# Decoder layer on one core: rotated queries and keys spread to head slots by four SBUF-to-SBUF transfers a group instead of four ScalarE copies

## The chip, the cores and the metric

The kernel is written directly in engine instructions and runs on 1 core of one Trainium2 chip. TensorE (PE), VectorE (DVE), ScalarE (ACT), GpSimd (POOL) and SyncE (SP) each run a list of their own and meet at semaphores. SP issues most transfers. The metric is the device time in microseconds of one execution; less is better.

## The reference, cut to what matters

128 sequences of 64 tokens with 128 features go through self-attention with rotary positions (16 heads of 8 dimensions, causal), cross-attention without softmax, and a feed-forward part that sends every token to one of 8 experts. Only the first part is touched:

```python
qkv = x @ qkv_w.T + qkv_b                       # after a layer norm of x
q, k, v = (qkv[0], qkv[1], qkv[2])              # 16 heads x 8
q = apply_rope(q, cos, sin)                     # pairs dimension d with d + 4 of its head
k = apply_rope(k, cos, sin)
scores = jnp.einsum('bhqd,bhkd->bhqk', q, k) / math.sqrt(Hd)
scores = jnp.where(causal, jnp.finfo(scores.dtype).min, scores)
attn = jax.nn.softmax(scores, axis=-1)
out = jnp.einsum('bhqk,bhkd->bhqd', attn, v)
```

## The kernel before

The 8192 tokens are cut into 32 groups of 256 (NG = 32). A first part runs over groups as a pipeline: every engine has a function `one(g)`, which lists its steps for one round, and `stage(g, k, step)` runs a step for group g - k. So in round r the first steps work on group r and the last ones on group r - 8. Within an engine the list is fixed, and a step that waits holds up all behind it. Nearly every tile is double (`two(...)`), chosen by the parity of the group. A second part runs 71 blocks of 128 rows through the experts; in it PE is the busiest engine. Nothing of this second part is changed.

For one group the front of the pipeline is: load `xin` (SP, `load_x`), row statistics (DVE, `stats_x`), scale (POOL `std_x`, ACT `norm_x`), turn (PE, ACT `xT`), queries and keys (PE `queries_keys`, L661), bias and rotation factors (DVE `rotate`, L1389), exchange of the rotary partners between partitions (DVE `partners`, L1399), and the difference `qk` (POOL `rotated`, L1885). `qk` is 128 x 512: features on partitions, 256 tokens of queries and 256 of keys.

A matmul for scores takes a strip of 32 partitions, that is four heads. To tell the heads apart, one operand is `ex`, 128 x 4 x 512: slot i holds the rows of `qk` that belong to head i of their strip, and zeros elsewhere. Before the change ACT makes it with four instructions a group (`by_head`, L1048), each a copy of the whole `qk` scaled by a column of zeros and ones (`own4`). Slots 2 and 3 are made one ACT round later than 0 and 1. PE reads `ex` in `max_scores` (L690, whose row maxima DVE takes at L1409) and in `scores` (L723); L728 adds the shifts and ACT takes the exponential (`exp`, L1064, `prob`).

SP's list for a round is `load_x` of group r, `load_ctx` of group r, `load_again` of group r - 3, then late constants in the first rounds, the mask in round 4 (`LOAD_AT`) and an expert weight of 256 KB in each of rounds 10 to 25. The three loads wait for the buffer to be free: `load_x` for `norm_x` of two groups before, `load_ctx` for the turn of the context (L755), `load_again` for `x1`.

POOL's list for a round is `std_x`, `std_y` (L1931 to L1935), `divide` (L1900), `rotated` (L1885), `max_low` (L1892), two indirect stores of rows (`scatter_rows`, L1980, which wait for the slot numbers `sli` that DVE makes at L1603 after `turned_back` at L1432 and `scaled_scores` at L1494), `std_x2` (L1948 to L1952), `row_scalars`, `offset_x1` (L1923), `std_x1` (L1911 to L1916), `gain` (L1940) and `scaled_affinity` (L1970).

Of the kernel before, what the change touches and what calls it, by code (L numbers as in the profile page):

```python
# [35 lines left out]
P = 128  # L36
# [108 lines left out]
def decoder_kernel(nc, x, ctx, mask, wself, wcross, bcol, brow, cent, w1t, lngb, b1c, w2t, b2r,  # L145
# [17 lines left out]
    with es:  # L163
# [10 lines left out]
        ws = sb("ws", [P, 6, D])  # L174
        WQ, WQR, WK, WKR, WV, WO = (ws[:, i, :] for i in range(6))
        wcx = sb("wcx", [P, 4 * D + E])
# [19 lines left out]
        o += P  # L196
        own4, own4s = cf[:, o:o + 4], cf[:, o + 4:o + 8]
        o += 8
# [144 lines left out]
        ac_l = stage_steps("act_norm_x", "n")  # L343
        ac_f = stage_steps("act_front", "xT | V0 V1 | x0 x1 x2 x3 | hi")
        ac_a = stage_steps("act_exp", "e0 | e1")
# [15 lines left out]
        d_xr = [sem(f"dma_x_again{i}") for i in range(2)]  # L361
        d_c = [sem(f"dma_ctx{i}") for i in range(2)]
        d_s = [sem(f"dma_scatter{i}") for i in range(2)]
        d_ident = sem("dma_identity")
# [15 lines left out]
        s_gain = sem("setup_routing_weights")  # L380
        s_turn = sem("setup_turned_weights")
        s_masks = sem("setup_scalar_masks")
        s_pads = sem("pad_rows_known")
# [76 lines left out]

        N_CONST, N_BIAS, N_LATE, N_WEIGHTS = 3, 10, 4, 2 * E
        LOAD_AT, WEIGHTS_AT = 4, 10
# [14 lines left out]
        def _(sp):  # L477
# [47 lines left out]
            def load_ctx(g):  # L525
# [4 lines left out]
                             ).then_inc(d_c[g.par], 16)  # L530

            def one(g):
                stage(g, 0, load_x)
                stage(g, 0, load_ctx)
                stage(g, 3, load_again)
# [38 lines left out]
        def _(pe):  # L574
# [80 lines left out]
            def queries_keys(g):  # L655

                first(pe, g, s_centre, 1)
                wait(pe, ac_f, g.n, "xT")
                free(g, "queries_keys")
                for i, w in enumerate((WQ, WK)):  # L660
                    last = mm(BANK["queries_keys"][:, i * TG:(i + 1) * TG], w, xT[g.par][:, :], start=True, stop=True)  # L661
                last.then_inc(*pe_f.done("QK"))
                if g.n == 1:
                    constants()
# [10 lines left out]
            def max_scores(g):  # L675

                first(pe, g, s_zero, 4)
                first(pe, g, s_masks, 1)
                for r_ in range(4):
                    free(g, f"max_scores{r_}")  # L680
                    half_ = slice(64 * (r_ % 2), 64 * (r_ % 2) + 64)
                    mm(quad[:, r_, :], ii[half_, :, :].rearrange("p b k -> p (b k)"), negq_b[half_, :],
                       start=True, stop=False, tile_position=(64 * (r_ % 2), 0))
                wait(pe, ac_f, g.n, "x3")
                for j in range(J):
                    for b in range(2):
                        own = slice((2 * j + b) * SQ, (2 * j + b + 1) * SQ)
                        for r_ in range(4):
                            strip = slice(32 * r_, 32 * r_ + 32)
                            last = mm(quad[64 * b:64 * b + 64, r_, 256 * j:256 * j + 256],  # L690
                                      qk[g.par][strip, 0, own], ex[g.par][strip, :, 1, own],
                                      start=False, stop=j == J - 1, tile_position=(32 * r_, 64 * b))
                            if j == J - 1 and b == 1:
                                last.then_inc(*pe_s.done(f"s{r_}"))
# [15 lines left out]
            def scores(g):  # L710
# [4 lines left out]
                for r_ in range(4):  # L715
                    free(g, f"scores{r_}")
                wait(pe, ac_f, g.n, "x3")
                for j in range(J):
# [269 lines left out]
        def _(ac):  # L988
            act, cp = nc.scalar.activation, nc.scalar.copy

            def masks():

                ac.wait_ge(d_rope, 32)
                cp(bvx[:, :], bc[:, 5:6].broadcast_to((P, P)))
                cp(pick[0:64, :, :, :].rearrange("p c b k -> p (c b) k"),
                   identf[0:64, 0:64].unsqueeze(1).broadcast_to((64, 8, SQ)))
                ac.wait_ge(d_const, 16 * N_CONST)
                for i in range(2):
                    cp(shift[i][0:64, :, :, :].rearrange("p j i q -> p (j i) q"),
                       nkf[0:64, :].unsqueeze(1).broadcast_to((64, 4 * J, SQ)))  # L1000
                cp(tri_b[:, :], trif)
                cp(negq_b[:, :].rearrange("p (h k) -> p h k", k=SQ),
                   nqf[:, :].unsqueeze(1).broadcast_to((P, 512 // SQ, SQ))).then_inc(s_masks, 1)
# [26 lines left out]
            def max_by_head(g):  # L1030
# [8 lines left out]
                last.then_inc(*ac_s.done("x"))  # L1039

            def by_head(g, part_):

                first(ac, g, d_const, 16 * N_CONST)
                wait(ac, pe_s, g.n - 2, "s3")
                wait(ac, pe_a, g.n - 2, "s3")
                wait(ac, po_f, g.n, "qk")
                for i in part_:
                    act(ex[g.par][:, i, :, :].rearrange("p a t -> p (a t)"),  # L1048
                        qk[g.par][:, :, :].rearrange("p a t -> p (a t)"), ACT.Copy, scale=own4[:, i:i + 1]
                        ).then_inc(*ac_f.done(f"x{i}"))  # L1050

# [130 lines left out]
            def one(g):  # L1182
                stage(g, 3, by_head, (2, 3))
                stage(g, 5, norm_x1)
# [11 lines left out]
                stage(g, 6, token_ids)  # L1196
                stage(g, 2, by_head, (0, 1))
                stage(g, 3, exp, 0)
# [4 lines left out]
            ac.dma_start(cf[:, i0:i1], consts[:, i0:i1]).then_inc(d_ident, 16)  # L1203
            ac.dma_start(cf[:, 0:i0], consts[:, 0:i0]).then_inc(d_rope, 16)
            ac.dma_start(bc[:, :], bcol).then_inc(d_rope, 16)
            ac.wait_ge(s_pool, 1)
# [51 lines left out]
        def _(dv):  # L1258
# [112 lines left out]
            def stats_x(g):  # L1371
# [3 lines left out]
                if g.n == 0:  # L1375
                    identities()
                    dv.wait_ge(s_pe, 1)
                    v.tensor_tensor(ws[:, 0:5:2, :], ws[:, 0:5:2, :],
                                    M[0][:, 0:3 * D].rearrange("p (a d) -> p a d", d=D), ALU.subtract
                                    ).then_inc(s_centre, 1)  # L1380

            def rotate(g):

                first(dv, g, d_rope, 32)
                wait(dv, po_f, g.n - 2, "qk")
# [9 lines left out]
            def partners(g):  # L1395
# [4 lines left out]
                                 t2[g.par][:, :, :].rearrange("p a t -> p (a t)"),  # L1400
                                 [p ^ (HD // 2) for p in range(32)]).then_inc(*dv_f.done("sh"))
                if g.n == 1:
# [281 lines left out]
            def setup(i):  # L1684
# [15 lines left out]
                v.tensor_scalar(pen[:, :], pen[:, :], 0.0, 1.0, ALU.mult, ALU.add).then_inc(s_mask, 1)  # L1700

            rounds(one, NG + 4, early=setup)

# [155 lines left out]
        def _(po):  # L1859
# [19 lines left out]
            def rotated(g):  # L1879

                wait(po, ac_f, g.n - 2, "x3")
                wait(po, pe_s, g.n - 2, "s3")
# [119 lines left out]
            for k in range(2):  # L2002
                v.memset(sc[k][:, :, 2], 1.0)
            v.memset(ones_b[:, :], 1.0).then_inc(s_pool, 1)
            po.wait_ge(s_pool, 1)

# [130 lines left out]
```

## Time and profile before

| | |
|---|---|
| median of 3 runs | 604.65 us (603.29 to 607.4) |
| the profiled execution | 602.47 us |
| its span | 600.2 us |
| busy: PE, DVE, ACT, POOL | 528.8, 496.4, 492.7, 421.1 us |
| mean granted TensorE clock | 0.989 of full speed |
| moved by DMA | 35.35 MB, 59 GB/s |

The span is the time between the first and the last instruction of the trace; 2.27 us of the profiled execution lie around it. A start in the rows is counted from the start of the span. "idle before" in square brackets is the time for which the engine stood still before the first instruction of a row, with what ended it. SPq and ACTq are the issue of a transfer by the queue of SP and ACT.

### The profile page before, as it was taken

What the parts mean: (1) busy time and instruction counts of PE and PEld (TensorE: products, weight loads), DVE (VectorE), ACT (ScalarE), POOL (GpSimd) and SP (SyncE); (2) the same over time, 40 slices, a digit from 0 to 9 for tenths busy, and PEclk for the clock granted to TensorE, in tenths of its full rate; (3) what the DMA queues carried; (4) which work ended last, traced back from release to release, by engine and by line L of the source; (5) the groups of instructions that cost most, each with busy time, mean ns of one, the idle gap of its engine ahead of it and who ended that gap; (6) DMA issues with size and microseconds to landing.
All of it is one profiled execution on the core that took longest, in us unless ns stands there. A gap on an engine that the chain in (4) does not pass through costs nothing.

```text
span 600.2 us, 25006 instructions
## 1 busy us (share of the span) xinstructions
PE 528.8 (88%) x7951; PEld 410.0 (68%) x7951; DVE 496.4 (83%) x1762; ACT 492.7 (82%) x1358; POOL 421.1 (70%) x820
## 2 busy tenths in 40 slices
PE   2755999999999988999989999898879998999995
PEld 1533776666666666666666666666668898899994
DVE  3627899999999999999999999999768777777773
ACT  1735788988988888888888888888778797899993
POOL 1311568888888888888888888887757766555553
PEclk9996999999999999999999999999999999999999
DMA  5142112122122111232211211110301222322210
GB/s 150 41 57 52 29 35 63 43 58 55 56 78 88 57 55 56 66 92 63 56 56 57 59 52 39 38 38 22 86 21 56 70 64 72 98 74 67 68 53 14
DMA packets 55183, 35.35 MB, mean 59 GB/s; under 512 B 14977, under 2 KB 50434, under 8 KB 55057
## 3 DMA queue, kind: packets, MB, share of 16 engines
q1 hardware_dynamic: 50160, 24.44, 15.6%
q0 software_dynamic: 4320, 8.66, 4.3%
q8 instruction: 68, 1.11, 0.8%
q10 hardware_dynamic: 576, 0.66, 0.4%
q14 instruction: 59, 0.48, 0.3%
HBM read 24.46 MB, written 9.74 MB: 57 GB/s over the span
## 4 chain that ended last, share of the span: by engine, by line
POOL 31%; PE 29%; issue 22%; DVE 10%; ACT 2%; DMA 2%; DVEq 2%; POOLq 1%; SPq 0%; ACTq 0%
PE side L940 8%; POOL expert_rows L1980 6%; POOL pay L1952 4%; PE quad L925 4%; PE side L925 4%; POOL on L1900 3%; POOL rs_T L1914 3%; POOL x L1923 3%; POOL rs_L L1875 2%; DVE hT L1551 2%; PE side L661 1%; PE quad L909 1%; PE quad L690 1%; DMA mk<-in_mask 1%; POOL ve_L L1873 1%
## 5 line engine op out<-in xcount | busy, mean ns | idle before, releaser
L2013 POOL DMA_INDIRECT out<-yo,rb x71 | 70.1, 987 | 60.1 <-DVE yo L1757 53.8
L1980 POOL DMA_INDIRECT expert_rows<-pay,sli x64 | 65.5, 1024 | 33.9 <-DVE sli L1603 19.6
L1048 ACT ACTIVATE ex<-qk,cf 128x512 f32<-128x512 f32 x128 | 85.4, 721 | 0.1
L1409 DVE TENSOR_REDUCE mx<-quad 128x16 f32<-128x1024 f32 x64 | 77.5, 1219 | 4.5 <-PE quad L690 4.1
L940 PE MATMUL side<-w,hT 128*128 x568 | 76.8, 278 | 4.7 <-DVE hT L1551 3.1
L940 PEld LDWEIGHTS side<-w,hT 128*128 128x128 f32 x568 | 69.1, 192 | 7.6 <-issue 7.3
L1064 ACT ACTIVATE prob<-quad 128x1024 f32<-128x1024 f32 x64 | 65.8, 1032 | 3.0 <-PE quad L728 2.2
L1541 DVE TENSOR_SCALAR xh<-rb 128x128 f32<-128x128 f32 x71 | 25.2, 356 | 28.2 <-issue 23.3
L1088 ACT ACTIVATE xn<-x,mr,rs_T 128x128 f32<-128x128 f32 x64 | 28.1, 486 | 24.3 <-POOL mr L1916 24.1
L1161 ACT COPY w1b<-w 128x512 f32 x71 | 43.5, 615 | 0.3 <-issue 0.3
L1009 ACT ACTIVATE xn<-xin,rs_L 128x128 f32<-128x128 f32 x64 | 22.2, 394 | 24.8 <-POOL rs_L L1875 24.7
L1036 ACT ACTIVATE shift<-side,own_i 64x128 bf16<-64x128 f32 x128 | 36.1, 355 | 2.8 <-PE side L704 1.1
L925 PE MATMUL quad<-xhT,w1b 128*128 128x128 f32 x288 | 38.2, 276 | 0.0
L690 PE MATMUL quad<-ex,qk 32*64 32x256 f32 x1024 | 36.1, 387 | 1.5 <-ACT ex L1048 1.5
L742 PE MATMUL side<-prob,vau 128*32 128x64 f32 x2048 | 35.7, 221 | 1.9 <-ACT prob L1064 1.8
L925 PE MATMUL side<-xhT,w1b 128*128 128x128 f32 x280 | 37.2, 276 | 0.0
L723 PE MATMUL quad<-ex,qk 32*64 32x256 f32 x1024 | 36.4, 392 | 0.4 <-DVE vau L1307 0.4
L925 PEld LDWEIGHTS quad<-xhT,w1b 128*128 128x128 f32 x288 | 35.4, 193 | 0.1
L661 PE MATMUL side<-xT,ws 128*128 128x256 f32 x128 | 34.9, 397 | 0.6 <-ACT xT L1016 0.6
L1952 POOL TENSOR_TENSOR pay<-ve,half 128x4 f32<-128x4 f32 x32 | 33.3, 1041 | 2.7
L1169 ACT ACTIVATE bs<-rb 128x128 f32<-128x128 f32 x71 | 35.0, 493 | 0.0
L1139 ACT ACTIVATE xhT<-quad,gb 128x128 f32<-128x128 f32 x71 | 33.0, 465 | 2.0 <-PE quad L909 1.8
(270 smaller groups left out, 1634.1 us busy)
## 6 DMA issues: line engine op xcount, KB each, us to landing
rb<-expert_rows SPq DMA_DIRECT2D x71, 68.0 KB, 1.9
xin<-in_x SPq DMA_DIRECT2D x32, 128.0 KB, 3.3
cin<-in_ctx SPq DMA_DIRECT2D x32, 128.0 KB, 2.1
xr<-in_x SPq DMA_DIRECT2D x32, 128.0 KB
w<-in_w1t SPq DMA_DIRECT2D x8, 256.0 KB, 3.6
w<-in_w2t SPq DMA_DIRECT2D x8, 256.0 KB, 3.4
out<-yo,rb POOLq DMA_INDIRECT x71
expert_rows<-pay,sli POOLq DMA_INDIRECT x64, 2.9
```

The source lines that it names most:

```text
L661: last = mm(BANK["queries_keys"][:, i * TG:(i + 1) * TG], w, xT[g.par][:, :], start=True, stop=True)
L690: last = mm(quad[64 * b:64 * b + 64, r_, 256 * j:256 * j + 256], qk[g.par][strip, 0, own], ex[g.par][strip, :, 1, own], start=False, stop= ...
L723: mm(quad[64 * b:64 * b + 64, r_, 256 * j:256 * j + 256], qk[g.par][strip, 1, own], ex[g.par][strip, :, 0, own], start=j == 0, stop=False, ...
L925: last = mm(HT[u][c // 2][:, (c % 2) * P:(c % 2 + 1) * P], w1b[u][:, c * P:(c + 1) * P], xhT[u][:, :], start=True, stop=True)
L940: last = mm(YB[u][:, 0:D], hT[u][:, c, :], w2[:, bass.ds(e, 1), c, :], start=c == 0, stop=c == FC - 1)
L1048: act(ex[g.par][:, i, :, :].rearrange("p a t -> p (a t)"), qk[g.par][:, :, :].rearrange("p a t -> p (a t)"), ACT.Copy, scale=own4[:, i:i + ...
L1064: act(prob[g.par][:, 2 * h_:2 * h_ + 2, :], quad[:, 2 * h_:2 * h_ + 2, :], ACT.Exp).then_inc(*ac_a.done(f"e{h_}"))
L1161: cp(w1b[u][:, :], w1[:, bass.ds(e, 1), :].rearrange("p e f -> p (e f)")).then_inc(*ffn["act_w1"].done("act_w1"))
L1409: v.tensor_reduce(mx[g.par][:, 2 * h_:2 * h_ + 2, :], quad[:, 2 * h_:2 * h_ + 2, :].rearrange("p r (h k) -> p r h k", k=SQ), AX.X, ALU.max ...
L1952: v.tensor_tensor(px[:, :, C_RS:C_A + 1], ve2[g.par][:, :, :], half[:, :].rearrange("p (j a) -> p j a", a=2), ALU.pow).then_inc(*po_r.done ...
L1980: v.indirect_dma_start(out=rows, out_offset=bass.IndirectOffsetOnAxis(ap=sli[g.par][:, j:j + 1], axis=0), in_=pay[g.par][:, j, :], in_offs ...
L2013: v.indirect_dma_start(out=o_rows, out_offset=bass.IndirectOffsetOnAxis(ap=number, axis=0), in_=yo[b.c % 4][:, :], in_offset=None, bounds_ ...
```

## The change

The four ACT copies a group are taken out. SP issues four transfers a group instead: slot i of `ex` gets the partitions i, i + 4, i + 8, ... of `qk`, 32 rows of 2 KB each. For that the features of queries and keys are laid out in another order within each strip of 32: the dimension first and the head last, so that head i has the rows i, i + 4, ... The two weight matrices get this order when DVE subtracts their mean, the rotary partner is now 16 partitions away instead of 4, and the rotation factors and biases are loaded in the new order (ten transfers on ACT's queue instead of two). The zeros of `ex` are written once, at the start, one buffer by DVE and one by POOL.

```diff
@@ SP
+            def by_head(g):
+                first(sp, g, s_clear, 2)
+                wait(sp, pe_s, g.n - 2, "s3")
+                wait(sp, pe_a, g.n - 2, "s3")
+                wait(sp, po_f, g.n, "qk")
+                for i in range(4):
+                    sp.dma_start(ex[g.par][i:P:4, i, :, :], qk[g.par][i:P:4, :, :]).then_inc(d_by[g.par], 16)
             def one(g):
+                stage(g, 2, by_head)
                 stage(g, 0, load_x)
                 stage(g, 0, load_ctx)
                 stage(g, 3, load_again)
@@ PE: queries_keys, and max_scores and scores
-                for i, w in enumerate((WQ, WK)):
+                for i, w in enumerate((WQP, WKP)):
...
-                wait(pe, ac_f, g.n, "x3")
+                wait_dma(pe, d_by, g, 4)
@@ ACT
-            def by_head(g, part_):
-                first(ac, g, d_const, 16 * N_CONST)
-                wait(ac, pe_s, g.n - 2, "s3")
-                wait(ac, pe_a, g.n - 2, "s3")
-                wait(ac, po_f, g.n, "qk")
-                for i in part_:
-                    act(ex[g.par][:, i, :, :].rearrange("p a t -> p (a t)"),
-                        qk[g.par][:, :, :].rearrange("p a t -> p (a t)"), ACT.Copy, scale=own4[:, i:i + 1]
-                        ).then_inc(*ac_f.done(f"x{i}"))
...
-                stage(g, 3, by_head, (2, 3))
...
-                stage(g, 2, by_head, (0, 1))
...
-            ac.dma_start(cf[:, 0:i0], consts[:, 0:i0]).then_inc(d_rope, 16)
-            ac.dma_start(bc[:, :], bcol).then_inc(d_rope, 16)
+            for r_ in range(4):
+                own = slice(32 * r_, 32 * r_ + 32)
+                ac.dma_start(cf[own, 0:4 * SQ], consts[own, 0:4 * SQ].rearrange("(i m) c -> m i c", i=4)
+                             ).then_inc(d_rope, 16)
+                ac.dma_start(bc[own, 0:4], bcol[own, 0:4].rearrange("(i m) c -> m i c", i=4)).then_inc(d_rope, 16)
+            ac.dma_start(cf[:, 4 * SQ:i0], consts[:, 4 * SQ:i0]).then_inc(d_rope, 16)
+            ac.dma_start(bc[:, 4:6], bcol[:, 4:6]).then_inc(d_rope, 16)
@@ DVE: stats_x of group 0, partners, and the start
-                    v.tensor_tensor(ws[:, 0:5:2, :], ws[:, 0:5:2, :],
-                                    M[0][:, 0:3 * D].rearrange("p (a d) -> p a d", d=D), ALU.subtract
-                                    ).then_inc(s_centre, 1)
+                    for i, w in enumerate((WQP, WKP)):
+                        v.tensor_tensor(w.rearrange("p (r m i) -> p r i m", r=4, i=4),
+                                        ws[:, 2 * i, :].rearrange("p (r i m) -> p r i m", r=4, i=4),
+                                        M[0][:, i * D:(i + 1) * D].rearrange("p (r i m) -> p r i m", r=4, i=4),
+                                        ALU.subtract)
+                    v.tensor_tensor(WV, WV, M[0][:, 2 * D:3 * D], ALU.subtract).then_inc(s_centre, 1)
...
-                                 [p ^ (HD // 2) for p in range(32)]).then_inc(*dv_f.done("sh"))
+                                 [p ^ 16 for p in range(32)]).then_inc(*dv_f.done("sh"))
...
+            v.memset(ex[0][:, :, :, :], 0.0).then_inc(s_clear, 1)
@@ POOL: rotated, and the start
-                wait(po, ac_f, g.n - 2, "x3")
+                wait_dma(po, d_by, g.back(2), 4)
...
+            v.memset(ex[1][:, :, :, :], 0.0).then_inc(s_clear, 1)
```

Three places show what this does to the lists. The first is SP's list in two rounds of the middle of the first part, before:

```order
L514 DMA xin_1<-in_x 128x2x128 [waits act_norm_x_n]
L528 DMA cin_1<-in_ctx 128x2x128 [waits pe_cross_cT]
L521 DMA xr_0<-in_x 128x2x128 [waits dve_cross_x1]
L509 DMA w2<-in_w2t 128x512
L514 DMA xin_0<-in_x 128x2x128 [waits act_norm_x_n]
```

and after:

```order
L515 DMA xin_1<-in_x 128x2x128 [waits act_norm_x_n]
L529 DMA cin_1<-in_ctx 128x2x128 [waits pe_cross_cT]
L522 DMA xr_0<-in_x 128x2x128 [waits dve_cross_x1]
L510 DMA w2<-in_w2t 128x512
L540 DMA ex_0<-qk_0 32x512 [waits pool_front_qk,pe_attention_s0,pe_scores_for_max_s0]
L540 DMA ex_0<-qk_0 32x512 x3
L515 DMA xin_0<-in_x 128x2x128 [waits act_norm_x_n]
```

Each load of `xin` now stands behind the four transfers of the group two before, and so behind that group's `qk`. The second place is the head of ACT's list, before:

```order
L1202 DMA ws<-in_wself 128x768
L1203 DMA cf<-in_consts 128x128
L1204 DMA cf<-in_consts 128x384
L1205 DMA bc<-in_bcol 128x6
L1207 ACT_TABLE_LOAD
L1207 ACTIVATE ea_0<-half 128x1 [waits setup_pool]
```

and after:

```order
L1200 DMA ws<-in_wself 128x768
L1201 DMA cf<-in_consts 128x128
L1204 DMA cf<-in_consts 32x1x256
L1206 DMA bc<-in_bcol 32x1x4
...
L1207 DMA cf<-in_consts 128x128
L1208 DMA bc<-in_bcol 128x2
L1210 ACT_TABLE_LOAD
L1210 ACTIVATE ea_0<-half 128x1 [waits setup_pool]
```

Eight transfers more stand ahead of the table load and of ACT's first `norm_x`. The third place is ACT's list around the exponentials in the middle of the first part, before:

```order
L1036 ACTIVATE shift_1<-side,own_i 64x2x64 x4
L1123 COPY pay_0<-tok_i 128x2
L1048 ACTIVATE ex_0<-qk_0,cf 128x512 x2
L1064 ACTIVATE prob_1<-quad 128x1024
L1108 COPY av_1<-side 128x256
L1064 ACTIVATE prob_1<-quad 128x1024
L1048 ACTIVATE ex_0<-qk_0,cf 128x512 x2
L1088 ACTIVATE xn1_0<-x1_0,mr_0,rs_T_0 128x128 x2
```

and after:

```order
L1047 ACTIVATE shift_1<-side,own_i 64x2x64 x4
L1123 COPY pay_0<-tok_i 128x2
L1064 ACTIVATE prob_1<-quad 128x1024
L1108 COPY av_1<-side 128x256
L1064 ACTIVATE prob_1<-quad 128x1024
L1088 ACTIVATE xn1_0<-x1_0,mr_0,rs_T_0 128x128 x2
```

Two copies ahead of the first exponential and two behind the second are gone; the rest stands as it did.

## Rows read from the trace of the kernel before

**Rows 1.** The page, part 1: busy time, share of the span, instructions.

```profile
PE 528.8 (88%) x7951; PEld 410.0 (68%) x7951; DVE 496.4 (83%) x1762; ACT 492.7 (82%) x1358; POOL 421.1 (70%) x820
```

**Rows 2.** The chain of waits in order of time, 200 to 240 us: start, us, what.

```profile
203.31 0.74 issue
204.05 0.49 POOL expert_rows L1980
```

**Rows 3.** The timeline of POOL, L1885, first and last of 25: start, us, instruction.

```profile
100.84 1.27 POOL L1885 TENSOR_TENSOR qk<-t__0 128x512 f32<-128x512 f32 x1
...
404.01 1.27 POOL L1885 TENSOR_TENSOR qk<-t__0 128x512 f32<-128x512 f32 x1
```

**Rows 4.** Waits of POOL, 100 to 400 us: total, times, longest.

```profile
POOL expert_rows L1980 <- DVE sli L1603: 16.9, 20, 0.9
```

**Rows 5.** The timeline of one round, 201 to 212 us, all engines.

```profile
201.74 1.27 POOL L1885 TENSOR_TENSOR qk<-t__0 128x512 f32<-128x512 f32 x1
...
201.87 0.45 DVE L1432 STREAM_TRANSPOSE ont<-on 128x256 f32<-128x256 f32 x1 [0.24 <-POOL on L1900]
...
202.24 0.82 DVE L1494 TENSOR_TENSOR tm<-y,sc 128x48 f32<-128x48 f32 x1
...
205.12 1.33 ACT L1048 ACTIVATE ex<-qk,cf 128x512 f32<-128x512 f32 x2
...
208.56 1.34 ACT L1048 ACTIVATE ex<-qk,cf 128x512 f32<-128x512 f32 x2
...
209.16 0.48 DVE L1264 BATCH_NORM_STATS2 stat_L<-xin 128x6 f32<-128x128 f32 x2
...
210.10 0.66 PEld L690 LDWEIGHTS quad<-ex,qk 32*64 32x64 f32 x32 [0.42 <-ACT ex L1048]
...
210.70 0.73 POOL L1940 TENSOR_TENSOR yg<-y,br 128x256 f32<-128x256 f32 x1
...
210.89 0.58 DVE L1590 TENSOR_TENSOR rk<-rk,ohb 128x16 f32<-128x16 f32 x1
```

**Rows 6.** The page, part 5, and the waits for tile ex, 100 to 400 us.

```profile
L1048 ACT ACTIVATE ex<-qk,cf 128x512 f32<-128x512 f32 x128 | 85.4, 721 | 0.1
...
  PEld quad L690: 7.6, 20
```

**Rows 7.** The page, part 6 (KB, us to landing), and tile xin, 100 to 400 us.

```profile
cin<-in_ctx SPq DMA_DIRECT2D x32, 128.0 KB, 2.1
...
DMA to landing us min/median/max: 2.3/3.3/4.7
```

**Rows 8.** The timeline of the start, 0 to 38 us.

```profile
1.67 0.45 ACTq L1204 DMA_DIRECT2D cf<-in_consts  x1
...
2.63 1.28 ACT L1207 ACT_TABLE_LOAD   x1 [2.63 <-issue]
...
6.50 0.69 ACT L1009 ACTIVATE xn<-xin,rs_L 128x128 f32<-128x128 f32 x2 [2.37 <-POOL rs_L L1875]
...
7.08 2.87 SPq L493 DMA_DIRECT2D wop<-in_wself  x4
...
17.11 1.27 POOL L1885 TENSOR_TENSOR qk<-t__0 128x512 f32<-128x512 f32 x1
...
23.60 0.48 DVE L1264 BATCH_NORM_STATS2 stat_L<-xin 128x6 f32<-128x128 f32 x2
...
29.85 1.33 ACT L1048 ACTIVATE ex<-qk,cf 128x512 f32<-128x512 f32 x2
30.05 1.04 PE L728 MATMUL quad<-shift,pick 128*128 128x512 bf16 x4
...
35.84 1.27 POOL L1885 TENSOR_TENSOR qk<-t__0 128x512 f32<-128x512 f32 x1
```

**Rows 9.** The chain of waits in order of time, 37 to 60 us.

```profile
38.91 0.37 SPq L528
...
39.83 6.54 DMA mk<-in_mask
```

More of the change, by code:

```diff
@@ L174, in decoder_kernel @@
         ws = sb("ws", [P, 6, D])
-        WQ, WQR, WK, WKR, WV, WO = (ws[:, i, :] for i in range(6))
+        WQP, WKP, WV, WO = (ws[:, i, :] for i in (1, 3, 4, 5))
         wcx = sb("wcx", [P, 4 * D + E])
@@ L196, in decoder_kernel @@
         o += P
-        own4, own4s = cf[:, o:o + 4], cf[:, o + 4:o + 8]
         o += 8
@@ L343, in decoder_kernel @@
         ac_l = stage_steps("act_norm_x", "n")
-        ac_f = stage_steps("act_front", "xT | V0 V1 | x0 x1 x2 x3 | hi")
+        ac_f = stage_steps("act_front", "xT | V0 V1 | hi")
         ac_a = stage_steps("act_exp", "e0 | e1")
@@ L362, in decoder_kernel @@
         d_c = [sem(f"dma_ctx{i}") for i in range(2)]
+        d_by = [sem(f"dma_by_head{i}") for i in range(2)]
         d_s = [sem(f"dma_scatter{i}") for i in range(2)]
@@ L381, in decoder_kernel @@
         s_turn = sem("setup_turned_weights")
+        s_clear = sem("setup_cleared_heads")
         s_masks = sem("setup_scalar_masks")
@@ L459, in at @@
             return bank[1] if use in MOVED and g.n >= MOVED[use] else BANK[use]
-        N_CONST, N_BIAS, N_LATE, N_WEIGHTS = 3, 10, 4, 2 * E
+        N_CONST, N_BIAS, N_LATE, N_WEIGHTS, N_ROPE = 3, 10, 4, 2 * E, 10
         LOAD_AT, WEIGHTS_AT = 4, 10
@@ L716, in scores @@
                     free(g, f"scores{r_}")
-                wait(pe, ac_f, g.n, "x3")
+                wait_dma(pe, d_by, g, 4)
                 for j in range(J):
@@ L991, in masks @@
             def masks():
-                ac.wait_ge(d_rope, 32)
+                ac.wait_ge(d_rope, 16 * N_ROPE)
                 cp(bvx[:, :], bc[:, 5:6].broadcast_to((P, P)))
@@ L1377, in stats_x @@
                     dv.wait_ge(s_pe, 1)
-                    v.tensor_tensor(ws[:, 0:5:2, :], ws[:, 0:5:2, :],
-                                    M[0][:, 0:3 * D].rearrange("p (a d) -> p a d", d=D), ALU.subtract
-                                    ).then_inc(s_centre, 1)
+                    for i, w in enumerate((WQP, WKP)):
[4 more added lines that the diff above has]
+                    v.tensor_tensor(WV, WV, M[0][:, 2 * D:3 * D], ALU.subtract).then_inc(s_centre, 1)
             def rotate(g):
-                first(dv, g, d_rope, 32)
+                first(dv, g, d_rope, 16 * N_ROPE)
                 wait(dv, po_f, g.n - 2, "qk")
```

## The prediction, written before the run

> **What bounds the kernel now.** I read part 1 of the page first: PE, DVE and ACT are all busy for over 80% of the span and POOL for 70% [rows 1]. By these shares an edit that takes 85.4 us from ACT [rows 6] looks large. The shares are averages over two parts, so next I read the chain of waits in order of time. From about 100 us to the end of the first part it runs through POOL, round after round (the piece in rows 2 is that of an indirect store), joined only by short pieces of DVE. The period is the same for 24 rounds: (404.01 - 100.84) / 24 = 12.63 us [rows 3]. The waits of POOL in that stretch confirm it. It waits for one thing, the slot numbers ahead of the indirect stores, 16.9 us in 20 places, 0.84 us each [rows 4]. Of that 0.74 us is "issue", which the chain shows between the end of `sli` and the store [rows 2]. So POOL's own list sets the round, and ACT stands nowhere in it: each `on`, `qk` or `x` on POOL starts when the one before ends.
>
> Why DVE can't be early for `sli` is seen in one round. `tm` (L1494) handles 48 columns and takes 0.82 us; it starts at 202.24 and ends at 203.06, just when POOL's `qk` ends (201.74 + 1.27 = 203.01) [rows 5]. `rk` (16 columns, 0.58 us) ends at 211.47 beside the end of POOL's `yg`, 211.43 [rows 5]. DVE is held by POOL there, not by ACT.
>
> The stretch before 100 us is different: a chain through all engines, in which a delay of ACT's first work or of a load counts in full. In it stands also a wait for the mask, 6.54 us from its issue [rows 9].
>
> **ACT's copies go.** They end at 206.45 and 209.90 in the round shown [rows 5]. Who gains? PE waits 0.42 us for the second pair at 210.10 [rows 5], 7.6 us in all for 20 groups [rows 6]. The maxima that follow on DVE start only after `rk`, which POOL's `yg` holds until 211.47, so these 0.42 us end in slack. The first exponential can start some 0.5 us earlier, which again ends ahead of DVE work that waits for POOL. In the steady rounds I count 0 for all of it; the cover is POOL's list of 12.63 us.
>
> In the fill there is one place on the chain: the copies at 29.85 end at 31.18, while the first exponential needs only two of the four matmuls of L728, that is about 30.05 + 1.04/2 = 30.6 [rows 8]. **Gain 0.5 us** (0 to 0.6).
>
> **SP's four transfers, and what is queued behind them.** No row shows an SBUF-to-SBUF transfer. The nearest rows: an issue takes 0.45 us [rows 8], and I count 0.48 with the gap to the next, or 2.87/4 = 0.72 in a form of 32 partitions [rows 8]; from issue to landing 2.1 us for a lone 128 KB and 3.3 us (2.3 to 4.7) for `xin`, issued behind another [rows 7]. `qk` ends at 203.01. The four issues take until 204.9 (0.48 each, since the source and target are plain rows) or 205.9 (0.72). They land by 204.5 + 3.3 = 207.8. PE is free for `max_scores` at 210.10 - 0.42 = 209.7 [rows 5], so PE does not wait, and POOL's next `rotated` on the same buffer is 25 us away.
>
> The load of `xin` is the delicate one. Before, it ran a whole round ahead. Now it is issued at 204.9 and lands at 204.9 + 3.3 = 208.2. DVE reads it at 209.16 [rows 5]. The room is 0.9 us. Behind that come two reserves: DVE's `rk` would take about 0.2 instead of 0.58 if POOL did not hold it, 0.37 us, and DVE waits 0.24 us for `on` at 201.87 [rows 5]. So the round keeps 12.63 us while the time from the end of `qk` to the landed `xin` is under 6.15 + 0.6 = 6.75 us; I expect 5.2, with 4.0 and 7.6 as ends (1.9 + 2.1; 2.9 + 4.7). `load_ctx` and `load_again` have over a round of reserve. **Steady cost 0**, with a tail that I price as a rival.
>
> The Trainium skill (DMA: Bandwidth & Descriptors, Anatomy of one DMA) gives a fixed 2.0 us for a transfer of the GpSimd path plus bytes over 436 GB/s. By it a 128 KB load takes 2.3 us and `xin` would land at 207.2. The row of 3.3 us is above that, and the rows decide.
>
> **ACT's start.** The two loads at 1.67 us become ten. After them come the table load, 1.28 us, and an exponential of 0.20 us; then ACT idled 2.37 us until `norm_x` at 6.50 [rows 8]. This idle time is the cover. Eight pieces rearrange rows on the DRAM side to 32 partitions. The same form is on SP, `wop`, 0.72 us each; a plain one is 0.48. Table load at 1.67 + 8 x 0.72 + 2 x 0.48 = 8.39; `norm_x` at 8.39 + 1.28 + 0.22 = 9.9 instead of 6.5: **loss 3.4 us**. With 0.48 for all ten: 6.47 + 1.50 = 7.97, loss 1.5 us. I take 3.4, since the form is that of `wop`. The first `rotate` needs the last piece; it is issued by 8 us and lands within 4.7 us more, while `norm_x`, the turn, its copy and the matmuls of 9.9 us and later stand before `rotate`: covered.
>
> The same skill page (Why a DMA increments its semaphore by 16) says that a transfer uses as many engines, up to 16, as divide both slowest dimensions, and that on fewer engines the issuing queue writes the missing semaphore counts itself. By it the pieces (8 on the DRAM side) would be of the dear kind, like `wop` (4), and the head transfers (32) of the cheap kind, which fits the choice made above from rows.
>
> **The second load of the fill.** `qk` of group 0 ends at 18.38, and with it now starts the way to `xin` of group 2: 1.9 us of issues and 3.3 us to land, 23.6, exactly when DVE wants it (23.60) [rows 8]; both ends move with the 3.4 us. **Loss 0.2 us** (0 to 2.4, the latter with 0.72 an issue and 4.7 to land). The two clears of `ex` lie on DVE and POOL while both wait for the first load; 0. The split of the weight centring is three short DVE instructions for one and lies before `xT`; 0.
>
> **The mask.** It is on the chain, issued at 39.83 behind `load_ctx` at 38.91 [rows 9]. In its round SP now issues four transfers and `xin` before `load_ctx`. `qk` of that group is ready at 35.84 + 1.27 = 37.1 [rows 8], so they end about 39.5: the mask is issued 0.6 us later and finds 128 KB more ahead of it in the rings. **Loss 1.0 us** (0.5 to 1.7).
>
> **Sum.** 3.4 + 0.2 + 1.0 - 0.5 = +4.1 us; ends +1.4 (1.5 + 0 + 0.5 - 0.6) and +7.5 (3.4 + 2.4 + 1.7 - 0). Against the profiled execution this gives 602.47 + 4.1 = 606.6. That execution is 2.2 us under the median of the three runs, so against the median I say 604.65 + 4.1 = **608.8 us**, own range 606.0 to 612.2. A measurement of this kernel can't tell less than about 1%, 6 us, from no change.
>
> **Rivals.**
>
> *ACT counts after all.* If the 85.4 us matter, the first sign is PE's wait for `ex`: 7.6 us over 23 groups, at most 10.9 us over all. With the costs at the start: -10.9 + 4.1 = -6.8, 597.9 us. For it speaks PE's business of 88%; against it that POOL never waits for PE or ACT between 100 and 400 us. 0.06.
>
> *The start is hidden.* The pieces are issued in 0.48 us each or less, and the later wait for the mask takes up the rest. Then the sum is about +0.3 (0.8 - 0.5), 605 us. Against it: the mask's issue waits itself for a chain from the first group. 0.11.
>
> *The load of `xin` becomes the bound (slower).* If the way from the end of `qk` to landed data is over 6.75 us, each round is longer by the excess: DVE stands at `stats_x`, its `turned_back` and `sli` come late, then POOL's stores, then the next `qk`, which again starts the next load. At 7.6 us it is 0.9 us for each of 24 rounds, 21 us, with the start +25: 630 us. For it: four issues and four transfers of 64 KB stand ahead of the load, and single loads landed after 4.7 us before [rows 7]. Against: 1.5 us of room by the medians. 0.17.
>
> *The forecast*, between +1.4 and +7.5: 0.66.
>
> **How the numbers follow.** The range 603.8 to 617 holds the forecast, most of the hidden start and the mild end of the slow rival (up to 0.35 us a round); outside are the first rival with 0.06 and the dear end of the third with some 0.12. Faster by over 1% (under 598.6): 0.05. Slower by over 1% (over 610.7): 0.17 and the upper end of the forecast, 0.12, so 0.29. Same: 0.66.
>
> **What the profile after would show.** Right: ACT's table load at about 8.4 us and `norm_x` at 9.9; the period of L1885 in the steady rounds 12.63 still, with the chain on POOL; ACT's busy time down by 85 us with idle time in front of L1064 and L1088; no wait of DVE's first statistics for `xin` beyond the fill; the mask's issue about 4 us later. Wrong: DVE L1264 waiting for DMA `xin` in steady rounds, or a period under 12.5, which would mean that POOL was not the bound. The prediction fails most easily at the landing time of `xin` behind four SBUF transfers, of which the trace has no example.

## The result, and the profile after

The changed kernel takes 608.16 us (median of 13 runs, 607.4 to 610.35), the kernel before 604.93 us beside it (13 runs, 602.58 to 607.4). The ratio is 1.0058, 95% interval 1.004 to 1.0076: 3.2 us slower, inside what I called no change. The profiled execution took 608.5 us; its span is 606.5 us at a mean granted clock of 0.984.

The page of the kernel after, part 1 (busy time, share of the span, instructions), part 5 (two groups of ACT: busy time, mean ns, idle time before them with what ended it) and part 6 (KB, us from issue to landing), answers to [rows 1, 6, 7]:

```profile
PE 527.6 (87%) x7951; PEld 408.6 (67%) x7951; DVE 497.9 (82%) x1765; ACT 417.4 (69%) x1230; POOL 423.2 (70%) x821
...
L1064 ACT ACTIVATE prob<-quad 128x1024 f32<-128x1024 f32 x64 | 65.5, 1027 | 32.5 <-PE quad L739 32.5
...
L1088 ACT ACTIVATE xn<-x,mr,rs_T 128x128 f32<-128x128 f32 x64 | 28.1, 486 | 63.1 <-POOL mr L1923 61.6
...
xin<-in_x SPq DMA_DIRECT2D x32, 128.0 KB, 2.4
```

The same two groups of ACT in the page of the kernel before:

```profile
L1064 ACT ACTIVATE prob<-quad 128x1024 f32<-128x1024 f32 x64 | 65.8, 1032 | 3.0 <-PE quad L728 2.2
...
L1088 ACT ACTIVATE xn<-x,mr,rs_T 128x128 f32<-128x128 f32 x64 | 28.1, 486 | 24.3 <-POOL mr L1916 24.1
```

ACT is busy for 75 us less, and it spends the time waiting: 32.5 us ahead of the exponentials (L1064) instead of 3.0, and 63.1 us ahead of `xn` (L1088) instead of 24.3. The wait of POOL for the slot numbers in the kernel after, 100 to 400 us (total, times, longest), is that of [rows 4] to the tenth:

```profile
POOL expert_rows L1987 <- DVE sli L1609: 16.9, 20, 0.9
```

The timeline of POOL after, groups 0, 1, 2, 3, 6, 30 and 31 (start, us, instruction), shows when each `qk` starts; [rows 3, 8] are its counterparts:

```profile
20.95 1.27 POOL L1892 TENSOR_TENSOR qk<-t__0 128x512 f32<-128x512 f32 x1
29.29 1.27 POOL L1892 TENSOR_TENSOR qk<-t__1 128x512 f32<-128x512 f32 x1
39.24 1.27 POOL L1892 TENSOR_TENSOR qk<-t__0 128x512 f32<-128x512 f32 x1
66.08 1.27 POOL L1892 TENSOR_TENSOR qk<-t__1 128x512 f32<-128x512 f32 x1
106.93 1.28 POOL L1892 TENSOR_TENSOR qk<-t__0 128x512 f32<-128x512 f32 x1
...
410.46 1.28 POOL L1892 TENSOR_TENSOR qk<-t__0 128x512 f32<-128x512 f32 x1
422.93 1.27 POOL L1892 TENSOR_TENSOR qk<-t__1 128x512 f32<-128x512 f32 x1
```

In the kernel before the same groups stand at 17.11, 25.44, 35.84, 60.34, 100.84, 404.01 and 416.48 us. The differences are 3.84, 3.85, 3.40, 5.74, 6.09, 6.45, 6.45. So 5.74 us of the loss are there with group 3 already, 0.35 more come by group 6 and 0.36 by group 30; from group 6 to group 30 the period is (410.46 - 106.93) / 24 = 12.65 us against 12.63. The second part gives back 0.15 us.

The timeline of ACT after, 0 to 12 us, shows the first 3.8 us:

```profile
1.68 1.29 ACTq L1204 DMA_DIRECT2D cf<-in_consts  x1
3.00 0.69 ACTq L1206 DMA_DIRECT2D bc<-in_bcol  x1
3.72 0.68 ACTq L1204 DMA_DIRECT2D cf<-in_consts  x1
...
8.96 1.28 ACT L1210 ACT_TABLE_LOAD   x1 [8.96 <-issue]
...
10.37 0.68 ACT L1020 ACTIVATE xn<-xin,rs_L 128x128 f32<-128x128 f32 x2
```

Seven pieces took 0.68 to 0.69 us, the first 1.29. `norm_x` starts at 10.37 instead of 6.50 [rows 8] and now follows its own list without a wait. The timeline after, 38 to 62 us, shows the next 2.3 us:

```profile
40.59 2.38 SPq L540 DMA_DIRECT2D ex<-qk  x4
43.02 0.58 SPq L515 DMA_DIRECT2D xin<-in_x  x1
43.65 0.47 SPq L529 DMA_DIRECT2D cin<-in_ctx  x1
44.16 0.47 SPq L522 DMA_DIRECT2D xr<-in_x  x1
44.67 0.47 SPq L499 DMA_DIRECT2D mk<-in_mask  x1
...
51.33 1.22 DVE L1701 TENSOR_REDUCE pen<-mk 128x64 f32<-128x1024 int32 x1 [12.90 <-DMA mk<-in_mask]
...
56.01 0.29 PE L715 MATMUL side<-ident_b,mt 128*32 128x64 bf16 x4 [12.96 <-ACT mt L1058]
...
58.31 2.01 PE L734 MATMUL quad<-ex,qk 32*64 32x256 f32 x32
```

The mask is issued 4.84 us later than at 39.83 [rows 9], 1.44 more than the shift of `qk`. DVE stands 12.90 us for it (11.37 before), and PE with it: PE runs nothing from 43.05 to 56.01 us, and between 51 and 60 us the granted clock is 0.50, the lower of its two levels, 1.2 GHz. The 32 matmuls of L734 take 2.01 us there and 1.12 us in a steady round. In the profile of before, this quad took 1.74 us, since the clock was back earlier (0.88 over 54 to 57 us):

```profile
53.38 1.74 PE L723 MATMUL quad<-ex,qk 32*64 32x256 f32 x32
```

From the mask's issue to `qk` of group 3 it is 21.41 us, and 20.51 before: another 0.9.

A steady round is free. The timeline of one round after, 207 to 216 us, answers to [rows 5]:

```profile
207.98 1.28 POOL L1892 TENSOR_TENSOR qk<-t__0 128x512 f32<-128x512 f32 x1
...
209.34 2.38 SPq L540 DMA_DIRECT2D ex<-qk  x4
...
210.61 1.12 PE L734 MATMUL quad<-ex,qk 32*64 32x256 f32 x32
...
211.77 0.59 SPq L515 DMA_DIRECT2D xin<-in_x  x1
...
215.30 0.48 DVE L1267 BATCH_NORM_STATS2 stat_L<-xin 128x6 f32<-128x128 f32 x2
```

`qk` ends at 209.26. The load of `xin` is issued 2.5 us later. From issue to landing it takes 2.4 us in the median (2.3 to 3.9 over 100 to 400 us), which gives 214.2, a microsecond ahead of its reader. In 300 us DVE waits for it twice, 0.8 us in all.

### The profile page after: what moved, and what is told of

The parts are those of the page before. It is cut to its first block, busy times and chain, and to the rows that moved or that the text cites. A ratio compares the mean times of both kernels' runs of the same rounds, so it can differ in the third digit from the quotient of the medians.

```text
span 606.5 us, 24987 instructions
## 1 busy us (share of the span) xinstructions
PE 527.6 (87%) x7951; PEld 408.6 (67%) x7951; DVE 497.9 (82%) x1765; ACT 417.4 (69%) x1230; POOL 423.2 (70%) x821
## 4 chain that ended last, share of the span: by engine, by line
POOL 31%; PE 30%; issue 22%; DVE 9%; ACT 2%; DVEq 1%; ACTq 1%; DMA 1%; POOLq 1%; SPq 1%
PE side L951 8%; POOL expert_rows L1987 6%; POOL pay L1959 4%; PE quad L936 4%; PE side L936 4%; POOL on L1907 3%; POOL rs_T L1921 3%; POOL x L1930 3%; POOL rs_L L1882 2%; DVE hT L1557 1%; PE quad L920 1%; PE side L672 1%; PE quad L734 1%; PE side L753 1%; DMA mk<-in_mask 1%
## 5 line engine op out<-in xcount | busy, mean ns | idle before, releaser
L1064 ACT ACTIVATE prob<-quad 128x1024 f32<-128x1024 f32 x64 | 65.5, 1027 | 32.5 <-PE quad L739 32.5
L1088 ACT ACTIVATE xn<-x,mr,rs_T 128x128 f32<-128x128 f32 x64 | 28.1, 486 | 63.1 <-POOL mr L1923 61.6
L734 PE MATMUL quad<-ex,qk 32*64 32x256 f32 x1024 | 36.7, 395 | 0.4 <-DVE vau L1310 0.4
L936 PEld LDWEIGHTS side<-xhT,w1b 128*128 128x128 f32 x280 | 34.5, 193 | 0.2
```

What stands on the lines that cost most here:

```text
L734: mm(quad[64 * b:64 * b + 64, r_, 256 * j:256 * j + 256], qk[g.par][strip, 1, own], ex[g.par][strip, :, 0, own], start=j == 0, stop=False, ...
L936: last = mm(HT[u][c // 2][:, (c % 2) * P:(c % 2 + 1) * P], w1b[u][:, c * P:(c + 1) * P], xhT[u][:, :], start=True, stop=True)
L1064: act(prob[g.par][:, 2 * h_:2 * h_ + 2, :], quad[:, 2 * h_:2 * h_ + 2, :], ACT.Exp).then_inc(*ac_a.done(f"e{h_}"))
```

## The experiments

My theory after the result: the steady rounds pay nothing, because POOL's list sets them; the loss lies ahead of `qk` of group 3, in ACT's ten loads and in the mask's place. The rivals: the rounds do lose something (copies against transfers) that another effect hides; ACT's freed time is worth something once POOL is relieved; or the margin of `xin` is nearly used up.

**The start by itself.** The rotation factors and biases are laid out by the host in the new order, so that ACT needs two plain loads again; the head transfers stay. The excerpt is shortened (`...`), and the host's part is left out.

```diff
-            for r_ in range(4):
-                own = slice(32 * r_, 32 * r_ + 32)
-                ac.dma_start(cf[own, 0:4 * SQ], consts[own, ...].rearrange("(i m) c -> m i c", i=4))
-                ac.dma_start(bc[own, 0:4], bcol[own, 0:4].rearrange("(i m) c -> m i c", i=4))
-            ac.dma_start(cf[:, 4 * SQ:i0], ...); ac.dma_start(bc[:, 4:6], ...)
+            ac.dma_start(cf[:, 0:i0], consts[:, 0:i0]).then_inc(d_rope, 16)
+            ac.dma_start(bc[:, :], bcol).then_inc(d_rope, 16)
```

> The changed kernel with one part undone: rotation factors and biases lie in the new order already in DRAM, so ACT's queue issues two plain transfers instead of ten; all else as changed. Theory (the ten issues delay ACT's first norm_x from 6.50 to 10.37 us and this goes in full down the chain of the fill): 3.8 us less than the changed kernel, 608.2 - 3.8 = 604.4 us, with qk of group 0 again at 17.1 us. Rival (a later wait swallows the start): no change, 608.2 us.

Measured: 604.7 us (12 runs), ratio to before 0.9995, 0.9973 to 1.0017. The start costs 608.16 - 604.7 = 3.5 us, and with it undone nothing is left that can be told from the kernel before. The timeline of POOL, groups 0, 2, 3 and 31:

```profile
17.64 1.27 POOL L1887 TENSOR_TENSOR qk<-t__0 128x512 f32<-128x512 f32 x1
...
35.93 1.26 POOL L1887 TENSOR_TENSOR qk<-t__0 128x512 f32<-128x512 f32 x1
62.75 1.27 POOL L1887 TENSOR_TENSOR qk<-t__1 128x512 f32<-128x512 f32 x1
...
419.33 1.27 POOL L1887 TENSOR_TENSOR qk<-t__1 128x512 f32<-128x512 f32 x1
```

The 3.3 us gained at group 0 (20.95 - 17.64) are still there at group 2 (3.31), 3 (3.33) and 31 (3.60): no wait in between swallows them, so the rival of a hidden start is out.

**How much room `xin` has.** Two, and then six, more SBUF-to-SBUF transfers of 64 KB are issued between the head transfers and the load of `xin`, in groups 6 to 27, into tiles that are idle there. They add work that no one reads. SP and, ahead of `rotated`, POOL wait for the extra transfers of two groups before; no wait of POOL for them shows in either trace. The excerpt is shortened (`...`); 2 stands for 2 or 6.

```diff
                     sp.dma_start(ex[g.par][i:P:4, i, :, :], qk[g.par][i:P:4, :, :]).then_inc(d_by[g.par], 16)
+                if not 6 <= g.n < NG - 4:
+                    return
+                wait_for(sp, d_junk[g.par], (g.n - 6) // 2 * 16 * 2)
+                for k in range(2):
+                    to = (hT[g.par][k % 4:P:4, :, :]..., w1b[g.par][k % 4:P:4, :])[k // 4]
+                    sp.dma_start(to..., qk[g.par][k % 4:P:4, :, :]).then_inc(d_junk[g.par], 16)
@@ POOL: rotated
+                if 8 <= g.n < NG - 2:
+                    wait_for(po, d_junk[g.par], (g.n - 6) // 2 * 16 * 2)
```

> The changed kernel with two more SBUF transfers of the same kind (qk into a tile unused at that time) between the four head transfers and the load of xin, for groups 6 to 27 only. They push each load of xin by 2 x 0.6 = 1.2 us. In the changed kernel the data lands about 4.9 us after the end of qk and the room was worked out as 6.75 us. Theory: 4.9 + 1.2 = 6.1, inside the room, no change, 608.2 us. Rival (the load already stands at its limit): +1.2 us in each of 22 rounds, 634 us.

Measured: 608.73 us, ratio to before 1.0074 (1.004 to 1.0108), so as without them.

> The same with six more transfers, 6 x 0.6 = 3.6 us. Theory (a loop from qk over the load of xin, DVE's statistics and POOL back to qk, which costs only the excess over 6.75 us): 4.9 + 3.6 - 6.75 = 1.75 us in each of 22 rounds, +38 us, 647 us, with DVE waiting for xin in each round. Rival (the load has a round in reserve): no change. Rival (no room at all): +79 us, 687 us.

Measured: 658.01 us, ratio 1.0867 (1.0822 to 1.0912). The loss per round is 2.4 us: (436.11 - 120.67) / 21 = 15.02 us a round. The waits, 100 to 400 us, first of the kernel with two more and then of the one with six more:

```profile
DVE stat_L L1275 <- DMA xin<-in_x: 20.0, 20, 1.6
```

```profile
DVE stat_L L1275 <- DMA xin<-in_x: 59.2, 19, 4.9
...
POOL ve_L L1888 <- DVE mv_L L1278: 42.4, 19, 3.3
```

With two, DVE waits for the load in 20 rounds, 1.0 us each, and the period is still (409.97 - 106.46) / 24 = 12.65: the wait takes the place of waits for POOL. With six the wait goes through to POOL, which now stands for the statistics. One round of that kernel:

```profile
226.30 1.27 POOL L1902 TENSOR_TENSOR qk<-t__0 128x512 f32<-128x512 f32 x1
227.65 2.38 SPq L541 DMA_DIRECT2D ex<-qk  x4
230.08 2.51 SPq L547 DMA_DIRECT2D hT<-qk  x4
232.63 1.23 SPq L547 DMA_DIRECT2D w1b<-qk  x2
233.91 1.75 SPq L516 DMA_DIRECT2D xin<-in_x  x1
...
237.41 0.49 DVE L1275 BATCH_NORM_STATS2 stat_L<-xin 128x6 f32<-128x128 f32 x2 [2.04 <-DMA xin<-in_x]
240.99 1.28 POOL L1902 TENSOR_TENSOR qk<-t__1 128x512 f32<-128x512 f32 x1
```

From the end of `qk` (227.57) to the data it is 9.84 us, and from there to the next `qk` 3.58. Over all 21 rounds the first takes 9.5 to 11.1 us, 10.2 in the mean, and the second 3.57 us each time, give or take 0.01. In a round of 12.63 us there are 11.36 us between the end of one `qk` and the start of the next, so the room is 11.36 - 3.58 = 7.8 us. The changed kernel uses 4.9 in the round shown above, and that with two more 7.1 in the mean of 19 rounds (6.2 to 7.8). The loop that I priced as the slower rival is real. It begins 1 us further out than I put it, and it closes by another way: I had it go over DVE's late `sli` and POOL's stores, but POOL stands for `mv_L` ahead of `std_x`, and its waits for `sli` over 100 to 400 us fall from 16.9 to 9.3 us. The total is 11 us above the 647 that I expected, although the room is wider, because the way is 10.2 us and not 4.9 + 3.6 = 8.5. The eleven issues from the first head transfer to `xin` took 1.1 us more than their usual sum (2.38, 2.51, 1.23 and 0.58 us) in the mean of 20 rounds, and up to 2.3 us more. In the round shown it is the issue of `xin` that is long, 1.75 us; in others it is one of the transfers.

**Is ACT's time worth anything once POOL is relieved?** Two small sums on POOL's list (L1955 and L1956 of the kernel after) are made by ACT, once in the changed kernel and once in the kernel before with its copies. The excerpt is shortened (`...`).

```diff
@@ ACT
+            def variances(g):
+                wait(ac, po_r, g.n - 2, "pow")
+                wait(ac, dv_r, g.n, "a1")
+                act(ve2[g.par][:, :, 0], pay[g.par][:, :, C_V], ACT.Copy, bias=EPS)...
+                act(ve2[g.par][:, :, 1], pay[g.par][:, :, C_V], ACT.Copy, scale=1.0 + EPS, bias=EPS * EPS...)...
...
                 stage(g, 6, token_ids)
+                stage(g, 6, variances)
@@ POOL: std_x2
-                v.tensor_scalar(ve2[g.par][:, :, 0], px[:, :, C_V], EPS, None, ALU.add)...
-                v.tensor_scalar(ve2[g.par][:, :, 1], px[:, :, C_V], 1.0 + EPS, EPS * EPS, ALU.mult, ALU.add...)...
-                wait(po, po_r, g.n, "eps2")
+                wait(po, ac_v, g.n, "v1")
```

> The changed kernel with two of POOL's instructions on 128 x 2 elements (the two sums under the root in std_x2, 0.25 and 0.20 us, with their gaps 0.6 us a round) given to ACT, where the copies stood. Theory (POOL's own list sets the steady round): the period falls from 12.65 to 12.05 us, 25 rounds, -15 us, 593 us. Rival (PE, DVE or ACT sets the round): no change, 608 us; a mixed answer, a smaller fall, would mean that another engine takes over below 12.65 us.

> The kernel before with the same two POOL instructions given to ACT, which here still makes the four copies a group. In the changed kernel this move took the period from 12.65 to 11.96 us and 17.4 us off the whole. Theory (ACT, busy 10.9 us of a round of 12.63 before, still has room): the same -17.4 us, 604.7 - 17.4 = 587.3 us. Rival (the room on ACT that the change makes is what the move needs; with the copies ACT is late for POOL or PE): a gain of less than 12 us, over 592.5 us. By this rival the transfers are worth the difference.

Measured: 590.82 us (0.9773, 0.9741 to 0.9806) with transfers and 587.43 us (0.9708, 0.9667 to 0.9748) with copies. The difference of 3.4 us is that of the two kernels without the relief, 3.2. The periods are (405.10 - 106.06) / 25 = 11.96 and (389.93 - 103.02) / 24 = 11.95 us. In the changed kernel the two sums with their gaps fill 0.63 us of POOL's list (212.65 to 213.28 us). So taking 0.6 us off POOL's list takes 0.7 us off each round, which shows what sets it, and ACT carries the copies and the sums together at no cost.

**The mask's place.** It is issued two rounds earlier, in SP's round 2.

```diff
+                if i == 2:
+                    sp.dma_start(mk[:, :, :], m_rows).then_inc(d_mask, 16)
                 k = i - LOAD_AT
                 if k == 0:
-                    sp.dma_start(mk[:, :, :], m_rows).then_inc(d_mask, 16)
```

> The changed kernel with the transfer of the mask issued by SP in round 2 instead of round 4, behind the load of the context; all else as changed. Theory (the fill stands for the mask: DVE waits 12.9 us, from 38.4 to 51.3 us): the mask is there before DVE wants it and about 11 us go, 597 us. Rival (another chain of the fill is as long): no more than 3 us go, 605 us.

Measured: 595.2 us, 0.9839 (0.9798 to 0.988), 13.0 us under the changed kernel. Group 3 in the timelines of this kernel and of the kernel before:

```profile
51.49 1.27 POOL L1893 TENSOR_TENSOR qk<-t__1 128x512 f32<-128x512 f32 x1
```

```profile
60.34 1.27 POOL L1885 TENSOR_TENSOR qk<-t__1 128x512 f32<-128x512 f32 x1
```

14.6 us earlier than the changed kernel's 66.08, of which 13.0 arrive at the end. The mean clock is 0.995. The same move in the kernel with copies, between the two kernels `relief_with_copies` and `all_before`, gives 587.43 - 575.53 = 11.9 us. So the wait for the mask, whose issue the change puts off by 1.4 us more than `qk`, costs either kernel far more than the change does.

**All that helps, with transfers and with copies.** Mask in round 2 and POOL relieved in both; the kernel with transfers also has its plain start, so that head transfers and copies are what differs.

> The changed kernel with three edits together: plain start (-3.5 us measured), mask in round 2 (-11 us by the theory), and two POOL instructions on ACT (-17.4 us measured). Theory: the three lie in different stretches and add up, 608.4 - 31.9 = 576.5 us. Rival (once the fill is shorter PE sets its rounds and half of the mask's gain is given back): 582 us.

> The kernel before, with ACT's copies, and two edits: mask in round 2 and two POOL instructions on ACT. Theory (the copies cost nothing): within 2 us of the changed kernel with its three edits, about 577 us. Rival (ACT's room now counts): 5 us or more above it.

Measured: 575.99 us (573.63 to 576.75; 0.9523, 0.9492 to 0.9554) with transfers, 575.53 us (574.88 to 576.58; 0.9518, 0.9487 to 0.9549) with copies. Part 1 of the page of each:

```profile
PE 524.1 (92%) x7951; PEld 407.3 (71%) x7951; DVE 487.4 (85%) x1765; ACT 424.9 (74%) x1294; POOL 409.4 (72%) x757
```

```profile
PE 527.5 (92%) x7951; PEld 410.2 (72%) x7951; DVE 481.1 (84%) x1762; ACT 498.0 (87%) x1422; POOL 407.8 (71%) x756
```

73 us of ACT's busy time in, or out, and the times differ by less than their ranges. Both beat the kernel before by 4.8%, and neither owes that to the head transfers. The idea of the change is worth nothing that these runs can tell, in a tighter kernel too.

**The kernel before, profiled twice more.** One thing did not add up: the two profiled executions stand 6.0 us apart (6.3 by their spans), the medians 3.2. Two more profiles of the kernel before, unchanged, each of a single execution, on another chip than the experiments above:

> The kernel before, unchanged, profiled again. The shown profile of before took 602.5 us while its median is 604.9 us, and its distance to the profile of the changed kernel, 6.0 us, is larger than that of the medians, 3.2 us. Theory: executions of the kernel before differ in the fill, in the stretch between the landing of the mask and the fifth group, where the granted clock is at half; a slower one has qk of group 3 some 2 us later than 60.3 us and the same period of 12.63 us. Rival: the difference is spread over the steady rounds or the second part.

> The same, once more, since a single look may meet a fast execution again. Same expectations.

Measured: 605.86 us (span 603.6) and 604.73 us (span 602.5). Two windows of the first of them, 22 to 26 and 26 to 30 us (columns: stretch, its length, busy time and count of PE, PEld, DVE, ACT and POOL, granted clock, DMA share, GB/s), and what stands in its timeline there:

```profile
22.00:26.00 4.00, 3.13 (x34) 1.55 (x35) 3.89 (x19) 1.11 (x3) 1.31 (x3) 0.67 0.01 2
26.00:30.00 4.00, 3.94 (x29) 2.77 (x35) 3.09 (x18) 2.44 (x9) 1.09 (x2) 0.90 0.02 5
```

```profile
22.87 1.60 PE L690 MATMUL quad<-ex,qk 32*64 32x256 f32 x32 [1.83 <-ACT ex L1048]
24.41 2.08 PE L796 MATMUL side<-br,mean_m 128*128 128x512 f32 x2
```

In both the clock fell here, to 0.67 and 0.62 over 22 to 26 us; in the execution that I had worked from it stayed at 1.00, and the same quad stood so:

```profile
22.73 1.12 PE L690 MATMUL quad<-ex,qk 32*64 32x256 f32 x32 [1.46 <-ACT ex L1048]
```

`qk` of groups 0, 2, 3 and 6 stands at 17.25, 37.07, 62.33, 102.61 in the first and 17.42, 37.15, 62.15, 102.44 in the second. Against these the changed kernel is 3.7 and 3.5 us late at group 0, 2.2 and 2.1 at group 2, 3.8 and 3.9 at group 3, and 2.9 and 4.0 at the end of the span. The last two lie about the 3.2 of the medians. So the profile of before that I read was one of its quick executions, and against the others the kernel with transfers wins back 1.5 us between groups 0 and 2. All seven profiles of kernels with head transfers had a clock of 1.00 in 22 to 26 us, and three of the five with copies had not. In these five the clock goes with a wait: where the clock stayed at 1.00, PE had waited 1.46 and 1.38 us for ACT's copies ahead of this quad, and groups 0 to 2 took 18.73 us; where it was 0.62 to 0.67, the wait was 1.83, 2.02 and 2.08 us and groups 0 to 2 took 19.7 to 19.8. One of these three ran on the chip of the later experiments (`relief_with_copies`), so the other chip is not what makes the difference. In the seven kernels with head transfers the wait for the transfers was 0.9 to 1.6 us. That the longer wait leads to the lower clock fits all twelve but is only argued: no run changed that wait alone.

## Why the prediction was right, step by step

- **What bounds the kernel**: POOL's list, shown by 0.6 us of relief giving 0.7 us a round. ACT's copies were worth nothing in three pairs of kernels. Its busy time fell by 75 us and not by the 85 that I named, since the copies' rows overlap those of their neighbours; the waits came where I had put them, 29.5 us more ahead of L1064 and 38.8 more ahead of L1088. The 7.6 us in [rows 6] that I called a wait of PE are a wait of its weight loads (PEld).
- **ACT's start**, +3.4: the terms were 0.72 a piece and `norm_x` at 9.9. Measured 0.68, the first 1.29, and 10.37, so +3.8 at group 0 between the two profiles, and 3.5 us by the kernel with a plain start. The other bound, 0.48 us for every issue, was wrong, as was the rival that the mask's wait would take the loss up.
- **Two kinds of transfer**: by the Trainium skill (DMA: Bandwidth & Descriptors, Why a DMA increments its semaphore by 16) the issuing queue writes the missing counts itself when a transfer uses fewer than 16 engines. That this makes the pieces dear and leaves the head transfers cheap was my inference. The trace agrees on the pieces, 0.68 us against 0.45 for a plain load of the same queue, though no run shows that the missing counts are the reason. A head transfer took 0.60 us to issue (2.38 for four), between my 0.48 and 0.72.
- **Exponentials in the fill**, -0.5: the first one starts at 34.53 us, 0.5 earlier than 31.21 + 3.85, and 0.45 us show between groups 1 and 2 of the two profiles.
- **The second load of the fill**, +0.2: nothing. `stat_L` of group 2 starts at 27.45, which is 23.60 + 3.85, without a wait.
- **The mask**, +1.0: under-sized. It is issued 1.44 us later beyond the shift. I had counted 0.6, since I took 0.48 for a head transfer (0.5 us over four) and for the load of `xin` (0.58), and nothing for the gaps. What follows the mask's issue then took 0.9 us longer between the two profiles, 0.1 and 0.4 against the two further ones, in which the quad of L723 took 2.01 us as well. I had no term for that.
- **The steady rounds**, 0: 0.36 us over 24 rounds, as near as one execution tells. The way from the end of `qk` to the landed `xin` was 4.9 us (expected 5.2) and the room 7.8 (expected 6.75, on a path over `sli` that did not bind). The load landed in 2.4 us, not in the 3.3 of [rows 7], which I took for it. An estimate by the Trainium skill (DMA: Bandwidth & Descriptors, Anatomy of one DMA), 2.0 us plus the bytes over 436 GB/s, stated there for the GpSimd path, is 2.3 us for 128 KB. Here it was the better number.
- **The sum**, +4.1: 6.0 us between the two profiled executions and 3.2 between the medians. Against the two further profiles, in their mean, the start cost 3.6, groups 0 to 2 gave back 1.5 where I had 0.3 (0.5 - 0.2), and the mask with what follows it cost 1.7 where I had 1.0. That makes +3.8 at group 3; the 3.5 at the end of the span differ by less than the two profiles do from each other. So the mechanism was right, and that the forecast of 608.8 came as near to 608.16 as it did is in part luck: two errors of opposite sign, 1.2 and 0.7 us, nearly cancel, and the first of them could not be seen in the execution that I read.

## What to carry to other kernels

A busy share of 82% on an engine is no reason to relieve it: find which list sets the round and ask whether the engine stands in the chain there, since here 0.6 us a round off POOL's list gave 17 us in all while 73 us off ACT's gave nothing. When a queue gets a step that waits for a late result, list every load behind it and measure its room from that result to its reader, and count the issues ahead of an engine's first work one by one. A single wait of 12 us in the fill can be worth more than the change in hand: moving one load two rounds ahead gave 13 us.

## What the runs showed of the hardware

- PE's clock in the fill differed between executions of one and the same kernel: 1.00, 0.67 and 0.62 of full speed over 22 to 26 us. With it groups 0 to 2 took 18.73, 19.82 and 19.73 us.
- After the wait for the mask (no PE work for 13.0 us) the clock was at the lower level, and the quad of 32 matmuls took 2.01 us instead of 1.12.
- An SBUF-to-SBUF transfer of 32 rows of 2 KB took 0.60 us of SP's time to issue. The four of group 0 were issued from 22.32 to 24.77 us, and PE, which waited for them, started at 26.15.
- The issue of the load of `xin` took 0.43 us in the median before and 0.59 behind head transfers. Single issues are longer: 1.68 us once in 23 before, 1.24 to 2.08 in 4 of 23 after.
- The small load behind the mask's issue (`gb`) took 4.48 us to issue, and 0.57 us where the mask had gone out two rounds earlier:

```profile
45.18 4.48 SPq L501 DMA_DIRECT2D gb<-in_lngb  x1
```
